# One of every two router row tiles is normalized on GpSimd instead of ScalarE

## The chip, the cores and the metric

One core of a Trainium2 chip. The metric is the device time of one execution in microseconds (us), taken as the median of several executions. Everything is float32.

## The reference, cut to what matters

The input is 4 x 1024 tokens of 256 values. It is layer-normalized, and the result feeds two branches, whose outputs are added to the input:

```python
xn = _layernorm(x, axis=-1)                     # (x - mean) / sqrt(var + eps)
x = x + attn(xn, ...) + ffn(xn, Wr, W1, V1, W2)
# attn: RMS norm, two projections 256 -> 512, a causal convolution of 4 taps, silu,
#       h = exp(d * A) * h + (d * x) * b over 1024 steps (512 channels x 16 states), y = sum(h * c),
#       gate, projection 512 -> 256, plus its own residual
# ffn:
gates = softmax(xn @ Wr)                        # 8 experts
_, inds = top_k(-gates, 2)                      # the two smallest gates of each token
out = (silu(xn @ W1[e]) * (xn @ V1[e])) @ W2[e] # for the two chosen e, weighted by their scores
```

The change concerns the rows `xn` that the router and the experts read.

## The kernel before, in words

**Chunks and units.** The tokens are worked on in 16 chunks of 256. Each chunk has 32 "units" (2 halves of the channels x 16 states). For a unit w, ScalarE computes two exponentials (`exps`, L547 to L555), VectorE one product (`products`, L1133) and two scans (`scan`, L1149), GpSimd once for every two units a product of 128x1024 (`parts`, L758), and TensorE adds these up (`sum_parts`, L850). ScalarE issues the exponentials of unit w + 2 at unit w, GpSimd takes the pair w - 2, w - 1 at an even unit w, and TensorE sums unit w - 4 at unit w.

**Pieces.** All other work is cut into pieces, written by hand into tables (`B_PLACES`, `F_PLACES` and others) that say after which unit of the chunk a piece comes. Every engine walks the same tables in its own instruction order, some kinds of piece some units later (`LATER`): the router pieces `R` come on GpSimd one unit later and on SyncE two units later than on ScalarE and TensorE. An engine executes its instructions strictly in its own order, and a wait holds up everything behind it.

**The router pieces.** Chunk 0 has 18 pieces `R` 0 to 17, at the places `[1, 3, 5, 10, 11, 13, 15, 17, 19, 23, 25, 26, 26, 26, 26, 26, 27, 29]`. Of the 32 row tiles of 128 tokens, piece i (i < 16) handles tiles 2i and 2i + 1:

- ScalarE (L669 to L683) normalizes the two tiles from `xall` into two of the four slots of `tok` (L676), and then copies the turned tiles 2i - 2 and 2i - 1 from the banks H and V into `xT` (L682).
- TensorE (L974 to L991) multiplies the tiles 2i - 4 and 2i - 3 by the router's weights (L982, 8 columns into bank X), and then turns the tiles 2i - 2 and 2i - 1 from `tok` into the banks H and V (L990). It waits for `xn_r`, the count of normalized tiles.
- GpSimd (L776 to L786) computes the residual rows of the tiles 2i and 2i + 1 from the same `xall` (L785).
- SyncE (L467 to L477) stores the two tiles of `tok` to the DRAM tensor `xt` (L473, after `xn_r`) and the two residual tiles to `acc` (L476, after `res_set`).

A slot of `tok` is used again by piece i + 2, which therefore waits until TensorE has turned the tiles of piece i (the bank count of piece i + 1) and until the store of piece i has landed (`xt_out`). A residual slot waits in the same way for `res_out`.

**What follows them.** When all 32 tiles have their 8 logits, VectorE computes gates, choices and slots (pieces RA to RE, L1170 to L1258), and SyncE loads the experts' weights (L480, L483) over the memory of `xall`. Also in chunk 0 the pieces B of chunk 1 are made: ScalarE's taps (L610, L612) and GpSimd's two additions for each of four channel groups (L793, L795; ScalarE's next taps wait for the second), the silu (L617), the projections B3 (L908, L910), B4 (L920, read by ScalarE at L638 and L640).

Of the kernel before, what the change touches and what calls it, by code (L numbers as in the profile page):

```python
# [18 lines left out]
ALU = mybir.AluOpType  # L19
ACT = mybir.ActivationFunctionType  # L20
# [199 lines left out]
def mamba_moe(nc, x, norm_w, skip_wT, in_wT, conv_w, conv_b, wd1T, wd2T, wd2_b, wBCT, A_log, W_D, out_wT,  # L220
# [3 lines left out]
    with ctx:  # L224
# [144 lines left out]
        s_part = sem("s_part")  # L369
        s_sum = sem("s_sum")  # L370
        y_taken = sem("y_taken")
        xn_r = sem("xn_r")
        xTr = sem("xTr")
        lgt = sem("lgt")
# [53 lines left out]
        @block.sync  # L428
        def _(sp):
            def load_quarter(t):  # L430
                sp.dma_start(xall[:, t:t + 8, :], x_rows[t * P:(t + 8) * P, :].rearrange("(t p) d -> p t d", p=P)).then_inc(ld_x[t // 8], 16)

            def load_chunk(c):

                if c >= 1:
                    wait_full(sp, "G", ("B1", 0, c - 1))
                sp.dma_start(xch[:, :, :], x_rows[c * CH:(c + 1) * CH, :].rearrange("(s p) d -> p s d", p=P)).then_inc(ld_xch[c % 2], 16)

            def load_rows(k):

                c, q, n = unit(2 * k)
                if k >= ROW_PAIRS:
                    sp.wait_ge(s_part, k - ROW_PAIRS + 1)
                if q == 0 and n == 0:
                    sp.wait_ge(brow_w, 32 * (c + 1))
                sp.dma_start(bcr[:, k % ROW_PAIRS * 2:k % ROW_PAIRS * 2 + 2, :],
                             brow_d[N * c + n:N * c + n + 2, :].unsqueeze(0).to_broadcast([P, 2, 2 * CH])).then_inc(ld_bc[k % ROW_PAIRS], 16)

            def do(piece):
                kind = piece[0]  # L450
                if kind == "B1" and piece[2] + 1 < CHUNKS:
                    load_chunk(piece[2] + 1)
                elif kind == "B3":
                    c = piece[2]
                    wait_taken(sp, "G", piece)
                    for k in range(2):
                        sp.dma_start(brow_d[N * c:N * (c + 1), k * CH:(k + 1) * CH], tap[N * k:N * (k + 1), 0, :]).then_inc(brow_w, 16)
                    if c == 0:
                        load_rows(0)
                        load_rows(1)  # L460
                elif kind == "T5":
                    c = piece[2]
                    for s, b in enumerate("HG"):
                        t = SUB * c + s
                        wait_taken(sp, b, ("T3", 0, c))
                        sp.dma_start(out_rows[t * P:(t + 1) * P, :], mst[:, s, :]).then_inc(o_out, 16)
                elif kind == "R" and piece[1] < TT // 2:  # L467
                    i = piece[1]
                    if i == 0:
                        sp.wait_ge(zero_set, 1)  # L470
                        sp.dma_start(xt[TOKENS:TOKENS + P, :], empty).then_inc(xt_zero, 16)
                    sp.wait_ge(xn_r, 2 * (i + 1))
                    sp.dma_start(xt[2 * i * P:2 * (i + 1) * P, :].rearrange("(s p) d -> p s d", p=P),  # L473
                                 tok[:, 2 * i % 4:2 * i % 4 + 2, :]).then_inc(xt_out[i % 2], 16)
                    sp.wait_ge(res_set, 2 * (i + 1))
                    sp.dma_start(acc[2 * i * P:2 * (i + 1) * P, :].rearrange("(s p) d -> p s d", p=P),  # L476
                                 resid[i % 2]).then_inc(res_out[i % 2], 16)  # L477
                elif kind == "R" and piece[1] == TT // 2:

                    sp.dma_start(v1[:, :].rearrange("p (e k f) -> p e k f", e=EXPERTS, k=KD), V1.rearrange("e (k p) f -> p e k f", p=P)).then_inc(ld_v1, 16)  # L480
                    sp.wait_ge(xn_r, TT)
                    sp.wait_ge(res_set, TT)
                    sp.dma_start(w1[:, :].rearrange("p (e k f) -> p e k f", e=EXPERTS, k=KD), W1.rearrange("e (k p) f -> p e k f", p=P)).then_inc(ld_w1, 16)  # L483
                elif kind == "MF":

                    sp.wait_ge(idx_set, 2)
                    sp.dma_start(w2[:, :].rearrange("p (e k f) -> p e k f", e=EXPERTS, k=FF // P), W2.rearrange("e (k p) f -> p e k f", p=P)).then_inc(ld_w2, 16)
                elif kind == "CP":
                    t0, t1 = ((0, TT - 2 * SUB), (TT - 2 * SUB, TT - SUB))[piece[1]]
                    wait_landed(sp, ("FC", JT))  # L490
                    wait_landed(sp, ("O3", 1, CHUNKS - 3 + piece[1]))
                    sp.dma_start(out_rows[t0 * P:t1 * P, :], acc[t0 * P:t1 * P, :]).then_inc(o_out, 16)
                elif kind == "LL":
                    wait_landed(sp, ("FC", JT))
                    wait_full(sp, "G", ("FA", JT))
                    sp.dma_start(last, acc[(TT - SUB) * P:TT * P, :].rearrange("(s p) d -> p s d", p=P)).then_inc(ld_last, 16)

            load_chunk(0)

            for done, loads in (  # L500
                (ld_first, [(inw[:, :, :], in_wT.rearrange("(k p) e -> p k e", p=P)),
                            (cw[:, :, :], conv_w.rearrange("(k p) w -> p k w", p=P)), (cb[:, :], conv_b)]),
                (ld_small, [(wbc[:, :, 0:N], wBCT[0].rearrange("(k p) n -> p k n", p=P)),
                            (wbc[:, :, N:2 * N], wBCT[1].rearrange("(k p) n -> p k n", p=P)),
                            (Am[:, :, :], A_log.rearrange("(k p) n -> p k n", p=P)),
                            (wd1[:, :, :], wd1T.rearrange("(k p) r -> p k r", p=P)),
                            (wd2[:, :], wd2T), (db[:, :], wd2_b), (WD[:, :], W_D)]),
            ):
                for dst, src in loads:
                    sp.dma_start(dst, src).then_inc(done, 16)  # L510
            for t in range(0, TT, 8):
                load_quarter(t)
            for dst, src in [(wrt[:, :, :], Wr.rearrange("(k p) e -> p k e", p=P)),
                             (outw[:, :, :], out_wT.rearrange("(k p) d -> p k d", p=P)),
                             (skw[:, :, :], skip_wT.rearrange("(k p) e -> p k e", p=P)),
                             (trim, tri), (csts, cst)]:
                sp.dma_start(dst, src).then_inc(ld_late, 16)
            for piece in prologue():
                do(piece)
            at = places_of("SP")  # L520
            for w in range(UNITS):
                if w % 2 == 0 and w // 2 + 2 < UNITS // 2:
                    load_rows(w // 2 + 2)
                for piece in at[w]:
                    do(piece)
            for piece in epilogue():
                do(piece)
            sp.wait_ge(o_out, 16 * 4)
# [3 lines left out]
        def _(act):  # L532
# [40 lines left out]
            def do(piece):  # L573
# [95 lines left out]
                elif kind == "R":  # L669
                    i = piece[1]  # L670
                    if i < TT // 2:
                        if i >= 2:
                            wait_full(act, "V", ("R", i - 1))
                            act.wait_ge(xt_out[i % 2], 16 * (i // 2))
                        for t in (2 * i, 2 * i + 1):
                            nc.scalar.activation(tok[:, t % 4, :], xall[:, t, :], ACT.Identity, bias=nmr[:, t:t + 1],  # L676
                                                 scale=rstd[:, t:t + 1]).then_inc(xn_r, 1)
                    if 1 <= i <= TT // 2:
                        for k, t in enumerate((2 * i - 2, 2 * i - 1)):
                            wait_full(act, "HV"[k], piece)  # L680
# [62 lines left out]
        def _(pool):  # L743
# [30 lines left out]
            def do(piece):  # L774
                kind = piece[0]
                if kind == "R" and piece[1] < TT // 2:  # L776
                    i = piece[1]
                    if i == 0:
                        pool.wait_ge(stat, STAT_LN[1])
                        for k in range(TT // 8):  # L780
                            pool.wait_ge(ld_x[k], 16)
                    at_least(pool, res_out[i % 2], 16 * (i // 2))
                    for k in range(2):
                        t = 2 * i + k
                        nc.gpsimd.tensor_scalar(resid[i % 2][:, k, :], xall[:, t, :], r1[:, t:t + 1], nmr[:, t:t + 1],  # L785
                                                ALU.mult, ALU.add).then_inc(res_set, 1)  # L786
# [60 lines left out]
        def _(pe):  # L847
# [30 lines left out]
            def do(piece):  # L878
# [95 lines left out]
                elif kind == "R":  # L974
# [10 lines left out]
                    if 1 <= i <= TT // 2:  # L985
                        for k, t in enumerate((2 * i - 2, 2 * i - 1)):
                            wait_free(pe, "HV"[k], piece)
                            pe.wait_ge(xn_r, t + 1)
                            for kd in range(KD):
                                mm = pe.transpose(bank["HV"[k]][:, kd * P:(kd + 1) * P], tok[:, t % 4, kd * P:(kd + 1) * P], idn[:, :])  # L990
                            mm.then_inc(full["HV"[k]], 1)  # L991
# [409 lines left out]
```

## Time and profile before

| | |
|---|---|
| median of 3 executions | 1282.13 us (1279.8 to 1283.07) |
| the profiled execution | 1284.09 us |
| its span, first to last instruction | 1282.3 us |
| mean granted TensorE clock | 0.926 of full speed |
| busy share: TensorE, VectorE, ScalarE, GpSimd | 84%, 91%, 79%, 78% |

PE is TensorE, PEld its weight loads, DVE is VectorE, ACT is ScalarE, POOL is GpSimd, SP is SyncE with its DMA queue. `scr` is the memory that holds `tok`, `xT`, the residual rows and others; `w` on the input side of L676 and L785 is `xall`. Times in the rows are from the start of the span.

### The profile page before, as it was taken

To read this page: it belongs to the slowest core of one execution; us is meant where nothing else is said; L and a number is where in the kernel's file an instruction comes from. 1 tells how busy PE (TensorE), PEld (TensorE's weight loads), DVE (VectorE), ACT (ScalarE), POOL (GpSimd) and SP (SyncE) were. 2 spreads that over 40 slices of the span, in tenths; PEclk is the share of its full clock that TensorE was granted. 3 is DMA by queue.
4 is the path that set the end of the run, shared out by engine and by line. 5 is a ranking of instruction groups with operands and counts; after the bars stand their busy time and mean duration, and the time that the engine had idled before them with its cause. 6 is when DMAs were issued, how large, how long until landed. Compare 5 with 4: busy or idle time off the path is not lost.

```text
span 1282.3 us, 20051 instructions
## 1 busy us (share of the span) xinstructions
PE 1073.0 (84%) x5406; PEld 807.0 (63%) x5406; DVE 1170.8 (91%) x2145; ACT 1013.4 (79%) x2153; POOL 1003.4 (78%) x602
## 2 busy tenths in 40 slices
PE   3379376587998989999989999898999999998766
PEld 2268265465766666676767666676767667675555
DVE  5874899899999999999989899999989899999896
ACT  2797345589898888879888898889888898988862
POOL 1396277678898979888888988989898988989654
PEclk8686597799999999899999999999999999999987
DMA  7467723745554453545545454555545455545436
GB/s 227 143 205 253 267 77 106 231 139 146 147 146 140 141 160 120 150 141 145 146 133 155 121 154 138 146 157 144 146 123 155 135 145 148 155 122 140 126 125 190
DMA packets 87117, 195.08 MB, mean 152 GB/s; under 512 B 11184, under 2 KB 47152, under 8 KB 86928
## 3 DMA queue, kind: packets, MB, share of 16 engines
q1 hardware_dynamic: 69008, 171.18, 41.4%
q0 software_dynamic: 17712, 22.55, 10.6%
q8 instruction: 47, 0.77, 0.2%
q14 instruction: 62, 0.51, 0.1%
q10 hardware_dynamic: 288, 0.07, 0.0%
HBM read 171.22 MB, written 26.48 MB: 154 GB/s over the span
## 4 chain that ended last, share of the span: by engine, by line
PE 32%; ACT 21%; POOL 17%; issue 13%; DVE 12%; DMA 4%; DVEq 0%; POOLq 0%; ACTq 0%
POOL part L763 11%; ACT aexp L554 8%; PE yps L858 7%; PE bankX L1051 5%; DVE hb L1159 5%; PE bankV L1041 4%; PE bankH L1017 4%; DVE bps L1138 4%; DMA acc<-scr,idx 3%; ACT tap L612 3%; ACT L554 2%; PE bankG L898 1%; POOL scr L771 1%; POOL acc L819 1%; POOL tap L793 1%
## 5 line engine op out<-in xcount | busy, mean ns | idle before, releaser
L763 POOL TENSOR_TENSOR part<-hb,bcr 128x1024 f32<-128x1024 f32 x256 | 625.2, 2449 | 147.1 <-DVE hb L1159 102.5
L1159 DVE TENSOR_TENSOR_SCAN hb<-aexp,carry,bps 128x256 f32<-128x256 f32 x768 | 545.6, 733 | 11.4 <-ACT aexp L554 11.4
L554 ACT ACTIVATE aexp<-delta,Am 128x256 f32<-128x256 f32 x1024 | 446.9, 503 | 54.2 <-DVE hb L1159 52.7
L858 PE MATMUL yps<-idn,part 128*128 128x128 f32 x2048 | 300.2, 287 | 92.8 <-POOL part L763 88.4
L858 PEld LDWEIGHTS yps<-idn,part 128*128 128x128 f32 x2048 | 250.9, 148 | 164.9 <-POOL part L763 97.7
L1138 DVE TENSOR_TENSOR bps<-ups,bcr 128x512 f32<-128x512 f32 x512 | 345.2, 674 | 1.1
L1159 DVE TENSOR_TENSOR_SCAN hb<-aexp,bps 128x256 f32<-128x256 f32 x256 | 167.8, 673 | 23.9 <-ACT aexp L554 23.3
L1051 PE MATMUL bankX<-w,scr 128*128 x568 | 143.2, 397 | 21.8 <-ACT scr L703 19.4
L1017 PE MATMUL bankH<-w,scr 128*128 x284 | 137.9, 608 | 2.1 <-issue 2.1
L1041 PE MATMUL bankV<-v,scr 128*128 x284 | 134.2, 595 | 4.7 <-ACT xin L603 3.3
L1051 PEld LDWEIGHTS bankX<-w,scr 128*128 128x128 f32 x568 | 107.8, 198 | 43.0 <-issue 29.8
L819 POOL DMA_INDIRECT acc<-scr,idx x71 | 114.2, 1609 | 22.4 <-ACT scr L713 7.9
L793 POOL TENSOR_TENSOR tap<-tap 128x512 f32<-128x512 f32 x56 | 78.4, 1400 | 10.3 <-ACT tap L612 10.0
L771 POOL DMA_INDIRECT scr<-xt,idx x71 | 72.3, 1018 | 12.4 <-issue 7.4
L1017 PEld LDWEIGHTS bankH<-w,scr 128*128 128x128 f32 x284 | 51.0, 195 | 42.6 <-issue 40.6
L1041 PEld LDWEIGHTS bankV<-v,scr 128*128 128x128 f32 x284 | 48.4, 190 | 40.3 <-issue 40.3
L612 ACT ACTIVATE tap<-xin,cw 128x256 f32<-128x256 f32 x168 | 72.5, 496 | 0.0
L713 ACT ACTIVATE scr<-bankX,meta 128x256 f32<-128x256 f32 x71 | 33.1, 466 | 49.1 <-PE bankX L1051 49.1
L1327 DVE SCALAR_TENSOR_TENSOR scr<-scr,bankH 128x512 f32<-128x512 f32 x71 | 47.5, 669 | 26.3 <-ACT scr L693 26.2
L693 ACT ACTIVATE scr<-bankH 128x512 f32<-128x512 f32 x71 | 41.9, 590 | 27.8 <-PE bankH L1017 27.8
L554 ACT ACT_TABLE_LOAD x48 | 61.6, 1283 | 0.9
L424 POOL TENSOR_TENSOR delta<-delta,y 128x1024 f32<-128x1024 f32 x15 | 35.3, 2355 | 33.3 <-ACT y L650 33.2
(187 smaller groups left out, 1616.9 us busy)
## 6 DMA issues: line engine op xcount, KB each, us to landing
bcr<-brows SPq DMA_DIRECT2D x256, 512.0 KB
w<-in_W SPq DMA_DIRECT2D x2, 4096.0 KB, 21.9
xch<-in_x SPq DMA_DIRECT2D x16, 256.0 KB, 3.8
w<-in_x SPq DMA_DIRECT2D x4, 1024.0 KB, 9.8
xt<-scr SPq DMA_DIRECT2D x16, 256.0 KB, 2.8
acc<-scr SPq DMA_DIRECT2D x16, 256.0 KB, 2.7
v<-in_V SPq DMA_DIRECT2D x1, 4096.0 KB, 14.9
acc<-mst POOLq DMA_DIRECT2D x15, 256.0 KB
```

Source lines behind the costliest of these rows:

```text
L554: nc.scalar.activation(aexp[:, w % EXP_SLOTS, i, :], delta[:, c % 2, e, :], ACT.Exp, scale=Am[:, e, n:n + 1]).then_inc(s_a, 1)
L612: ins = nc.scalar.activation(tap[:, w, :], xin[:, e, w:w + CH], ACT.Copy, scale=cw[:, e, w:w + 1])
L763: nc.gpsimd.tensor_tensor(part[:, slot:slot + 2, :, :], hb[:, state:state + 2, :, :], bcr[:, row:row + 2, CH:2 * CH].unsqueeze(2).to_broad ...
L771: nc.gpsimd.indirect_dma_start(out=tok[:, j % 2, :], out_offset=None, in_=xt, in_offset=bass.IndirectOffsetOnAxis(ap=idx[:, j:j + 1], axis ...
L793: nc.gpsimd.tensor_tensor(tap[:, 0:2, :], tap[:, 0:2, :], tap[:, 2:4, :], ALU.add).then_inc(cvs, 1)
L819: nc.gpsimd.indirect_dma_start(out=acc, out_offset=bass.IndirectOffsetOnAxis(ap=idx[:, j:j + 1], axis=0), in_=tok[:, 2 + j % 2, :], in_off ...
L858: mm = pe.matmul(yps[:, s, i * P:(i + 1) * P], part[:, w % (2 * PART_PAIRS), i, s * P:(s + 1) * P], idn[:, :], start=(n == 0 and s == 0 an ...
L1017: mm = pe.matmul(bank["H"][:, :], xT[:, j % 2, k, :], w1[:, bass.ds(col + k * FF, FF)], start=(k == 0), stop=(k == KD - 1))
L1041: mm = pe.matmul(bank["V"][:, :], xT[:, j % 2, k, :], v1[:, bass.ds(columns[j] + k * FF, FF)], start=(k == 0), stop=(k == KD - 1))
L1051: mm = pe.matmul(bank["X"][:, 0:D], gT[:, k * P:(k + 1) * P], w2[:, bass.ds(columns[j] + k * D, D)], start=(k == 0), stop=(k == FF // P - 1))
L1138: v.tensor_tensor(bps[w % 2][:, :, :], ups[:, :, :], bcr[:, w % (2 * ROW_PAIRS), 0:CH].unsqueeze(1).to_broadcast([P, 2, CH]), ALU.mult).th ...
L1159: v.tensor_tensor_scan(hb[:, w % STATE_SLOTS, i, :], aexp[:, w % EXP_SLOTS, i, :], bps[w % 2][:, i, :], first, ALU.mult, ALU.add).then_inc ...
```

## The change

ScalarE normalizes only tile 2i of a piece. GpSimd normalizes tile 2i + 1, ahead of the two residual tiles of the same piece, after the same two waits for the slot. A new semaphore `xn_p` counts GpSimd's tiles, and those who waited for `xn_r` now wait for both.

```diff
@@ SyncE, piece R
-                    sp.wait_ge(xn_r, 2 * (i + 1))
+                    sp.wait_ge(xn_r, i + 1)
+                    sp.wait_ge(xn_p, i + 1)
                     sp.dma_start(xt[2 * i * P:2 * (i + 1) * P, :].rearrange("(s p) d -> p s d", p=P),
@@ SyncE, the weight loads
-                    sp.wait_ge(xn_r, TT)
+                    sp.wait_ge(xn_r, TT // 2)
+                    sp.wait_ge(xn_p, TT // 2)
@@ ScalarE, piece R
-                        for t in (2 * i, 2 * i + 1):
-                            nc.scalar.activation(tok[:, t % 4, :], xall[:, t, :], ACT.Identity, bias=nmr[:, t:t + 1],
-                                                 scale=rstd[:, t:t + 1]).then_inc(xn_r, 1)
+                        t = 2 * i
+                        nc.scalar.activation(tok[:, t % 4, :], xall[:, t, :], ACT.Identity, bias=nmr[:, t:t + 1],
+                                             scale=rstd[:, t:t + 1]).then_inc(xn_r, 1)
@@ GpSimd, piece R
+                    if i >= 2:
+                        wait_full(pool, "V", ("R", i - 1))
+                        pool.wait_ge(xt_out[i % 2], 16 * (i // 2))
+                    t = 2 * i + 1
+                    nc.gpsimd.tensor_scalar(tok[:, t % 4, :], xall[:, t, :], rstd[:, t:t + 1], nmr[:, t:t + 1],
+                                            ALU.mult, ALU.add).then_inc(xn_p, 1)
                     at_least(pool, res_out[i % 2], 16 * (i // 2))
@@ TensorE, piece R
-                            pe.wait_ge(xn_r, t + 1)
+                            pe.wait_ge((xn_r, xn_p)[k], t // 2 + 1)
```

## Rows read from the trace of the kernel before

**Rows 1.** The page: busy time of each engine over the span

```profile
PE 1073.0 (84%) x5406; PEld 807.0 (63%) x5406; DVE 1170.8 (91%) x2145; ACT 1013.4 (79%) x2153; POOL 1003.4 (78%) x602
```

**Rows 2.** By stretch: busy PE, PEld, DVE, ACT, POOL; clock, DMA share, GB/s

```profile
65.40:85.10 19.70, 13.80 (x91) 12.50 (x89) 15.15 (x29) 18.92 (x45) 19.46 (x18) 0.83 0.52 173
85.10:103.10 18.00, 13.21 (x85) 10.34 (x85) 17.08 (x34) 17.97 (x44) 14.79 (x12) 1.00 0.85 276
103.10:128.10 25.00, 24.54 (x119) 22.81 (x118) 8.76 (x17) 18.45 (x44) 13.62 (x18) 0.52 0.78 244
160.00:240.00 80.00, 54.75 (x311) 48.21 (x309) 79.54 (x132) 42.93 (x84) 59.98 (x33) 0.86 0.31 98
```

**Rows 3.** Timeline of VectorE: start us, us, ..., idle before and releaser

```profile
103.25 0.67 DVE L1138 TENSOR_TENSOR bps<-ups,bcr 128x512 f32<-128x512 f32 x1
122.89 0.69 DVE L1159 TENSOR_TENSOR_SCAN hb<-aexp,bps 128x256 f32<-128x256 f32 x1 [12.60 <-ACT aexp L554]
128.27 0.42 DVE L1172 COPY w<-bankX 128x256 f32<-128x256 f32 x1 [3.51 <-PE bankX L982]
```

**Rows 4.** Timeline of ScalarE, 70 to 117 us

```profile
70.88 0.60 ACT L610 ACTIVATE tap<-xin,cb,cw 128x256 f32<-128x256 f32 x1 [0.75 <-POOL x L795]
73.38 1.08 ACT L676 ACTIVATE scr<-w,nmr,rstd 128x256 f32<-128x256 f32 x2
74.36 0.36 ACT L682 ACTIVATE scr<-bankH 128x256 f32<-128x256 f32 x1
81.74 0.38 ACT L682 ACTIVATE scr<-bankV 128x256 f32<-128x256 f32 x1
92.26 0.36 ACT L682 ACTIVATE scr<-bankV 128x256 f32<-128x256 f32 x1
114.85 1.09 ACT L676 ACTIVATE scr<-w,nmr,rstd 128x256 f32<-128x256 f32 x2 [1.17 <-DMA xt<-scr]
```

**Rows 5.** Line L785: duration ns min/median/max, first and last start us

```profile
L785 POOL TENSOR_SCALAR scr<-w,r,nmr x32: 554/560/577, 55.3 to 119.5; 128x256 f32<-128x256 f32 x32
```

**Rows 6.** Timeline of GpSimd, 70 to 125 us

```profile
70.11 0.73 POOL L795 TENSOR_TENSOR x<-tap 128x256 f32<-128x256 f32 x1
80.61 1.11 POOL L785 TENSOR_SCALAR scr<-w,r,nmr 128x256 f32<-128x256 f32 x2
84.01 1.11 POOL L785 TENSOR_SCALAR scr<-w,r,nmr 128x256 f32<-128x256 f32 x2
106.94 2.19 POOL L785 TENSOR_SCALAR scr<-w,r,nmr 128x256 f32<-128x256 f32 x4
122.95 2.36 POOL L763 TENSOR_TENSOR part<-hb,bcr 128x1024 f32<-128x1024 f32 x1 [2.86 <-PE yps L858]
```

**Rows 7.** Timeline of TensorE, 80 to 128 us

```profile
80.55 0.38 PE L990 MATMUL bankV<-idn,scr 128*128 128x128 f32 x2
85.92 1.97 PE L908 MATMUL bankG<-x,wd 128*128 128x256 f32 x8 [0.73 <-ACT x L617]
90.82 0.38 PE L990 MATMUL bankV<-idn,scr 128*128 128x128 f32 x2
91.04 1.04 PE L858 MATMUL yps<-idn,part 128*128 128x128 f32 x8
102.83 0.44 PE L990 MATMUL bankV<-idn,scr 128*128 128x128 f32 x2 [0.99 <-ACT delta L640]
110.43 1.88 PE L982 MATMUL bankX<-wrt,scr 128*128 128x8 f32 x8 [0.23 <-ACT scr L682]
124.62 0.63 PE L990 MATMUL bankV<-idn,scr 128*128 128x128 f32 x2
```

**Rows 8.** Timeline of SyncE's queue: the loads of the rows b and c

```profile
82.15 0.47 SPq L446 DMA_DIRECT2D bcr<-brows  x1
97.69 2.41 SPq L446 DMA_DIRECT2D bcr<-brows  x2
```

**Rows 9.** The chain of waits: the same projection L908 earlier, in chunk 0's prologue

```profile
25.21 3.68 PE bankG L908 x8
```

More of the change, by code:

```diff
@@ L371, in mamba_moe @@
         y_taken = sem("y_taken")
+        xn_p = sem("xn_p")
         xn_r = sem("xn_r")
```

## The prediction

> **What bounds the kernel now.** The page gives VectorE 91% of the span, the other three about 80% [rows 1]. The change touches 16 pieces between 54 and 122 us, so I read the busy times by stretch. Four stretches differ [rows 2]. From 65.4 to 85.1 us GpSimd is busy for 19.46 of 19.70 us and ScalarE for 18.92: both are full. From 85.1 to 103.1 ScalarE is full (17.97 of 18.00) and GpSimd has 3.2 us left. From 103.1 to 128.1 TensorE is full (24.54 of 25.00) at a granted clock of 0.52, that is at 1.2 GHz, while ScalarE has 6.5 us and VectorE 16 us to spare. After 160 VectorE is full (79.54 of 80). What links the third stretch to the rest is VectorE's first router instruction: it starts at 128.27 after waiting for the last logits on TensorE, and before that VectorE had stood 12.60 us waiting for ScalarE's exponentials, which lie behind the pieces R11 to R15 [rows 3]. So the date that matters is that of the last logits. Whatever it moves by moves VectorE's router work, and since VectorE then stays full, nearly the whole kernel. The question is what the change does to that date.
>
> **What is moved.** 16 instructions leave ScalarE. Two of L676 start 0.98 us ahead of what follows them (73.38 to 74.36 [rows 4]), so each takes 0.49 us of the engine, 7.8 us in all. 16 instructions come to GpSimd. They have the form of L785, a multiply and an add on 128x256 with one input tile; one takes 0.56 us alone [rows 5], and four in sequence take 2.19 [rows 6], so each after the first adds (2.19 - 0.56) / 3 = 0.54, 8.7 us in all. The price of the new instruction is thus known from the trace, with bounds of 0.55 and 0.58 for one alone [rows 5].
>
> A port rule speaks against the move. The 32 instructions L785 stand in stretches with VectorE scanning (to 109 us) and with it silent (110 to 122), and differ by 4% at most, 554 to 577 ns [rows 5]. The Trainium skill ("GPSIMD Engine Reference", Specifications) says that GpSimd's way into SBUF is shared with VectorE and contended when VectorE reads two SBUF inputs; by that rule the moved work would cost more than here. The trace of this stretch does not bear it out, and the kernel says why: scan and product each take one of their two inputs from PSUM.
>
> **Step 1, to R3.** R0 and R1 save ScalarE 0.98 us, but its time there ends in waits for TensorE's projection, so I count nothing. At R2 GpSimd's piece becomes 0.54 longer, and everything behind it in its order moves: the addition L795 from 70.11 [rows 6] to 70.65. ScalarE's next taps wait for exactly that one, 0.75 us in vain, until 70.88 [rows 4]; they start at 71.42. ScalarE's own saving at R2 only lengthens that wait. So ScalarE is 0.54 late, where one would expect it early. R3 gives 0.49 back: +0.05.
>
> **Step 2, R4 and R5: a new wait.** GpSimd has no gap here [rows 2], so R4 begins 2 x 0.54 later than 80.61 [rows 6], at 81.7, and its normalized tile is ready at 82.2. TensorE wanted to turn that tile (tile 9, bank V) at 80.55 [rows 7], and ScalarE to copy it at 81.74 [rows 4]. Now the turn starts at about 82.3 and takes 0.4, the copy starts at 82.75, and the exponentials behind it 0.26 later, at 83.0 instead of 82.0: ScalarE is 1.0 us late at this point, after having lost its savings of R4 and R5 (0.98) in the wait. Queued behind the waiting copy on ScalarE are the exponentials, VectorE's next input and the silu of chunk 1; VectorE loses about 1 us here and regains part, since it had other waits.
>
> **Step 3, R6 and R7.** GpSimd's R5 starts three additions later, 84.01 + 1.6 = 85.6 [rows 6], tile 11 is ready at 86.2. TensorE's R6 turns it by 86.65, then come two sums (x8, spacing 0.88 [rows 7]), so L908 starts at 87.5 instead of 85.92 [rows 7]. From the start of L908 to the end of R7's turn it takes 90.82 + 0.38 - 85.92 = 5.28 us [rows 7], so R7's bank V is ready at 92.8 and ScalarE copies it then, 0.55 later than 92.26 [rows 4].
>
> **Step 4, to the end of B4.** R8 gives 0.49 back: +0.05. GpSimd, 1.3 to 1.7 us late, has its gaps of 3.2 us in this stretch [rows 2] and is no longer in anyone's way: tile 15 is ready at 94.1, TensorE wants it at about 94. TensorE's turn for R9 into bank V waited until 102.83 for ScalarE's last read of B4 [rows 7], and moves with it by +0.05.
>
> **Step 5, R9 to R16.** Here TensorE works without a gap. Each piece costs it logits of 1.87 us and two turns, 2.9 us together. ScalarE's removed instructions (seven, 3.4 us) lie beside that and save nothing, except 0.2 us where TensorE waited 0.23 for a copy [rows 7]. The one wait for a store, 1.17 us until 114.85 [rows 4], delayed no TensorE work: TensorE is full all the same [rows 2]. GpSimd's new waits for `xt_out`: I walked R10 to R15 with landings 2.8 to 4.7 us after issue; the normalized tiles come at 108.3, 109.9, 111.7, 115.2, 117.7 and 119.9, each before TensorE turns it (the last one at 124.62 [rows 7]). The residuals of R15 end about 1 us later than before; the next product on GpSimd waited 2.86 us for TensorE, until 122.95 [rows 6], and covers that. Sum: +0.05 - 0.2, about -0.1 us at the last logits.
>
> **SyncE** waits for GpSimd's tile too, and behind these waits stand the loads of the rows. The tightest: the load at 82.15 [rows 8] moves with the residuals of R4 to 83.75, 5.0 us ahead of its use. In the kernel before the second load of the pair at 97.69 + 2.41 [rows 8] is used at 103.25 without a wait [rows 3], 3.15 us after the end of its issue. So nothing. The weight loads that follow R15 are first used in chunk 2 and stay hidden.
>
> **The sum.** The profiled execution took 1284.09 us; -0.1 gives 1284.0. That execution lies 1.96 above the median of 1282.13, so the forecast for the median is 1282.0. About 0.3% (3.9 us) is what a measurement of this kernel can tell from no change; three executions differ by 3.3 us.
>
> **Rival 1, ScalarE keeps its saving** (0.07). If GpSimd is not late at R2 to R5, the savings R3 to R8 reach B4: 6 x 0.49 = 2.9, with the 0.2 a gain of 3.1: 1279.0. For it: ScalarE is full to 103 [rows 2]. Against it: GpSimd's full stretch, and a row in which ScalarE already waits for L795 [rows 4].
>
> **Rival 2, the TensorE clock drops earlier** (0.14). With the new wait TensorE stands idle from about 80.5 to 82.3 and 85.0 to 86.2. If the clock falls to 1.2 GHz there, L908 takes 3.68 us [rows 9] instead of 1.97 [rows 7], L910 likewise +1.8, two sums +0.9, R7's logits and turns +1.4: 5.8 us. R7's bank V then comes at 98.6, ScalarE waits for it, and B4 and the last logits move by these 5.8 on top of the forecast: 1287.8, slower. If the clock is back after L908 the price is 2.6 and the result 1284.6, which I count as no change; it decides from 3.9 on, when the clock stays down through L910. For it: the clock was at 0.83 in this stretch, so it does fall there [rows 2]. Against: TensorE keeps 14 of 19.7 us of work, and the projections follow at once. I give 0.08 to the full price. The Trainium skill ("TensorE: Matmul & The Clock Gate", What's actually happening) has the slow clock as the default that only activity releases; more idling then makes the drop likelier, which is the direction of this rival.
>
> **Rival 3, the clock stays up through R9 to R16** (0.06). TensorE's 24.54 us [rows 2] of work at half clock would shrink, a piece from 2.9 to about 2.0 us (then ScalarE's copies and TensorE's latencies set it): 7 x 0.9 = 6: 1276, faster. The clock fell there after waits for ScalarE's L640 that the change leaves as they are.
>
> **Rival 4, GpSimd stays late** (0.12). If ScalarE can't take back its lateness since GpSimd's tiles of R7 and R8 come last as well, up to the 4 x 0.54 = 2.2 us of R2 to R5 reaches B4; less the 0.2 of step 5 that makes 1284.1, no change by the bound.
>
> The change does what it says; no case for it. The forecast itself has 0.61. Faster than 1278.3: rival 3 and the tail of rival 1, 0.08. Slower than 1286.0: rival 2 at full price and tails of rival 4, 0.12. Within: 0.80. The range 1278.5 to 1286.5 takes in rivals 1 and 4, the cheaper form of rival 2, and the spread of executions.
>
> **What would show it.** GpSimd's L785 and its new line 0.56 us each; ScalarE's taps at 71.4 with a wait of over 1 us for L795; a new wait for the new line on TensorE at 80 to 82 us and another at 85 to 86; GpSimd busy without a gap to 87; L908 at about 87.5; the last logits at 128.2 within 0.5. Wrong it would be if the first router instruction of VectorE starts before 126 or after 131, if TensorE's clock differs in 84 to 92 or 104 to 126, or if the time moves after 160 us, where I expect nothing.

## The result: slower, and the profile after

The changed kernel takes 1288.88 us (median of 13 executions, 1284.86 to 1293.63) against 1284.36 for the kernel before (13 executions, 1279.8 to 1287.6): ratio 1.0037, 95% interval 1.0024 to 1.0049, that is 4.5 us more. The forecast was 1282.0, no change, with a range up to 1286.5. It was wrong. Of the 6.9 us between forecast and result 2.2 come from the kernel before, whose first 3 executions had a median of 1282.13 and whose 13 have 1284.36; the change itself is the 4.5.

The page of the changed kernel gives nearly the same shares as [rows 1], with ScalarE's 6.9 us less and GpSimd's 8.5 us more; TensorE, which has the same instructions as before, is busy 14 us longer:

```profile
PE 1087.2 (84%) x5406; PEld 818.8 (64%) x5406; DVE 1169.7 (91%) x2145; ACT 1006.5 (78%) x2137; POOL 1011.9 (79%) x618
```

Busy time by stretch, in the columns of [rows 2], first the stretches of the forecast, then 72 to 92 us:

```profile
65.40:85.10 19.70, 13.96 (x69) 12.54 (x68) 13.55 (x26) 15.90 (x41) 19.39 (x20) 0.66 0.40 139
85.10:103.10 18.00, 17.55 (x103) 15.24 (x102) 14.78 (x29) 15.79 (x36) 17.35 (x18) 0.80 0.81 260
103.10:128.10 25.00, 22.23 (x104) 20.30 (x104) 11.66 (x24) 16.55 (x40) 17.70 (x25) 0.56 0.73 233
160.00:240.00 80.00, 55.50 (x308) 48.15 (x309) 79.19 (x132) 45.09 (x87) 59.14 (x32) 0.84 0.29 93
...
72.00:92.00 20.00, 17.49 (x79) 16.45 (x79) 13.06 (x26) 16.68 (x36) 19.77 (x21) 0.50 0.56 183
```

ScalarE, all but full before from 65 to 103 us, now has 6 us of gaps there. From 85.1 to 103.1 TensorE is full instead. And from 72 to 92 us its granted clock was 0.50 throughout, 1.2 GHz; in the kernel before it fell at 73 us and was back at 2.4 GHz from 80 on (the next two lines are of the kernel before):

```profile
72.00:80.00 8.00, 5.22 (x26) 5.22 (x26) 4.88 (x10) 8.00 (x21) 7.84 (x8) 0.57 0.49 162
80.00:92.00 12.00, 10.53 (x72) 8.15 (x72) 9.65 (x20) 11.94 (x25) 10.89 (x10) 1.00 0.64 212
```

**A common clock for the traces.** Executions reach the first product of GpSimd (L763, L766 after) between 52.9 and 54.5 us, whatever the kernel, so dates below that compare traces (30.1, 36.4) are counted from that product: 52.93 in the trace before, 54.12 after. The rows and the dates of the clock stay in us from the start of each span. L is the time from it to VectorE's first router instruction. The timeline of VectorE, after, answers to [rows 3]:

```profile
127.36 0.69 DVE L1168 TENSOR_TENSOR_SCAN hb<-aexp,bps 128x256 f32<-128x256 f32 x1 [12.86 <-ACT aexp L557]
...
133.04 0.42 DVE L1181 COPY w<-bankX 128x256 f32<-128x256 f32 x1 [3.82 <-PE bankX L991]
```

L is 133.04 - 54.12 = 78.9, before it was 128.27 - 52.93 = 75.3. So 3.6 us are there when the last logits are, beside 4.5 in the medians, and VectorE is full after 160 as before. An L comes from one execution. What follows it takes 1154.0 us in the trace before, 1155.4 after, and from 1148.5 to 1157.3 in the twenty traces, so an L can be set against an L, and not taken as a share of a median. Now the three timelines between. ScalarE after (L679 is the kept normalization, L685 the copies), answering to [rows 4]:

```profile
73.23 0.60 ACT L613 ACTIVATE tap<-xin,cb,cw 128x256 f32<-128x256 f32 x1 [1.77 <-POOL x L804]
...
83.24 0.38 ACT L685 ACTIVATE scr<-bankH 128x256 f32<-128x256 f32 x1 [0.74 <-PE bankH L999]
84.91 0.38 ACT L685 ACTIVATE scr<-bankV 128x256 f32<-128x256 f32 x1 [1.29 <-PE bankV L999]
...
96.43 0.38 ACT L685 ACTIVATE scr<-bankH 128x256 f32<-128x256 f32 x1 [2.15 <-PE bankH L999]
96.71 0.38 ACT L685 ACTIVATE scr<-bankV 128x256 f32<-128x256 f32 x1
...
106.64 0.58 ACT L679 ACTIVATE scr<-w,nmr,rstd 128x256 f32<-128x256 f32 x1
```

GpSimd after, with the new line L789, answering to [rows 6]:

```profile
83.51 0.56 POOL L789 TENSOR_SCALAR scr<-w,rstd,nmr 128x256 f32<-128x256 f32 x1
84.05 1.10 POOL L794 TENSOR_SCALAR scr<-w,r,nmr 128x256 f32<-128x256 f32 x2
85.11 2.36 POOL L766 TENSOR_TENSOR part<-hb,bcr 128x1024 f32<-128x1024 f32 x1
87.45 0.56 POOL L789 TENSOR_SCALAR scr<-w,rstd,nmr 128x256 f32<-128x256 f32 x1
```

TensorE after (L999 turns, L867 sums, L991 logits, L917 and L919 the projections of B3), answering to [rows 7]:

```profile
84.22 0.66 PE L999 MATMUL bankV<-idn,scr 128*128 128x128 f32 x2 [1.02 <-POOL scr L789]
84.67 1.91 PE L867 MATMUL yps<-idn,part 128*128 128x128 f32 x8
86.38 1.71 PE L991 MATMUL bankX<-wrt,scr 128*128 128x8 f32 x8
87.94 0.67 PE L999 MATMUL bankH<-idn,scr 128*128 128x128 f32 x2
88.40 0.63 PE L999 MATMUL bankV<-idn,scr 128*128 128x128 f32 x2
88.83 1.91 PE L867 MATMUL yps<-idn,part 128*128 128x128 f32 x8
90.53 2.76 PE L917 MATMUL bankG<-x,wd 128*128 128x256 f32 x8
...
96.23 0.38 PE L999 MATMUL bankV<-idn,scr 128*128 128x128 f32 x2
```

The story can be read off. TensorE waits 1.02 us for GpSimd's tile 9 and ScalarE 1.29 for its turn, as forecast. From then on TensorE has no gap until 96, but works at half clock: sums 1.91 us instead of 1.04, logits 1.71 instead of about 1. So the projection starts at 90.53, 3.4 us later than before on the common clock, and ScalarE, which arrives at R7 in good time, stands 2.15 us for the turns of R7. In ScalarE's queue behind them are the exponentials, B4 and R9.

### The profile page after: what moved, and what is told of

It reads as the page before. It is cut to its first block, busy times and chain, and to the rows that moved or that the text cites. A ratio compares the mean times of both kernels' runs of the same rounds, so it can differ in the third digit from the quotient of the medians.

```text
span 1288.4 us, 20081 instructions
## 1 busy us (share of the span) xinstructions
PE 1087.2 (84%) x5406; PEld 818.8 (64%) x5406; DVE 1169.7 (91%) x2145; ACT 1006.5 (78%) x2137; POOL 1011.9 (79%) x618
## 4 chain that ended last, share of the span: by engine, by line
PE 36%; POOL 21%; ACT 16%; issue 13%; DVE 10%; DMA 3%; DVEq 0%; POOLq 0%; ACTq 0%
POOL part L766 14%; PE yps L867 8%; ACT aexp L557 6%; PE bankX L1060 5%; PE bankH L1026 5%; PE bankV L1050 4%; DVE hb L1168 4%; DVE bps L1147 3%; DMA acc<-scr,idx 2%; ACT tap L615 2%; POOL tap L802 2%; POOL acc L828 2%; PE bankG L917 2%; PE bankG L919 1%; PE bankG L907 1%
## 5 line engine op out<-in xcount | busy, mean ns | idle before, releaser
L766 POOL TENSOR_TENSOR part<-hb,bcr 128x1024 f32<-128x1024 f32 x256 | 625.3, 2452 | 143.8 <-DVE hb L1168 98.6
L867 PE MATMUL yps<-idn,part 128*128 128x128 f32 x2048 | 305.9, 291 | 95.0 <-POOL part L766 91.2
L867 PEld LDWEIGHTS yps<-idn,part 128*128 128x128 f32 x2048 | 257.0, 151 | 167.3 <-POOL part L766 100.1
L1168 DVE TENSOR_TENSOR_SCAN hb<-aexp,bps 128x256 f32<-128x256 f32 x256 | 168.0, 674 | 25.5 <-ACT aexp L557 23.8
L774 POOL DMA_INDIRECT scr<-xt,idx x71 | 72.3, 1019 | 13.3 <-issue 7.7
L696 ACT ACTIVATE scr<-bankH 128x512 f32<-128x512 f32 x71 | 41.9, 589 | 30.2 <-PE bankH L1026 30.1
L425 POOL TENSOR_TENSOR delta<-delta,y 128x1024 f32<-128x1024 f32 x15 | 35.4, 2358 | 33.8 <-ACT y L653 32.8
```

The lines of the kernel that those rows point to most:

```text
L766: nc.gpsimd.tensor_tensor(part[:, slot:slot + 2, :, :], hb[:, state:state + 2, :, :], bcr[:, row:row + 2, CH:2 * CH].unsqueeze(2).to_broad ...
L774: nc.gpsimd.indirect_dma_start(out=tok[:, j % 2, :], out_offset=None, in_=xt, in_offset=bass.IndirectOffsetOnAxis(ap=idx[:, j:j + 1], axis ...
L867: mm = pe.matmul(yps[:, s, i * P:(i + 1) * P], part[:, w % (2 * PART_PAIRS), i, s * P:(s + 1) * P], idn[:, :], start=(n == 0 and s == 0 an ...
L1168: v.tensor_tensor_scan(hb[:, w % STATE_SLOTS, i, :], aexp[:, w % EXP_SLOTS, i, :], bps[w % 2][:, i, :], first, ALU.mult, ALU.add).then_inc ...
```

## The experiments

Three theories were set against each other: GpSimd's load in a full stretch (theory 1), TensorE's wait for GpSimd's tile (theory 2), and TensorE's clock, which stays at 1.2 GHz for longer (theory 3). `busy(n)` in the diffs issues n matmuls of 128x256 into columns of bank X that nothing reads at that time.

All are compared with the kernel before on the same chips; "time" is the median of 12 executions (6 for mid), the ratio is to the kernel before, with its 95% interval. The kernels of a set shared 23 to 35 executions of the kernel before, with medians between 1283.7 and 1284.3.

**load**: GpSimd's extra work alone.

```diff
+                    nc.gpsimd.tensor_scalar(resid[i % 2][:, 0, :], xall[:, 2 * i + 1, :], rstd[...], nmr[...],
+                                            ALU.mult, ALU.add).then_inc(twice, 1)
+                    pool.wait_ge(twice, i + 1)
                     for k in range(2):
```

> The kernel before, with GpSimd's part of the change as a load alone: it computes a tile like the moved one into the first residual slot, where the residual tile then overwrites it; ScalarE keeps both tiles and nobody waits for the extra one. Read as the local time L, from the start of GpSimd's first product to the start of VectorE's first router instruction: 75.3 us before, 78.9 after. If the load of a full GpSimd is the cause (theory 1), L rises by 3 us or more, since here not even ScalarE's saving counters it, and the whole by 3 to 6 us. If the new wait of TensorE for GpSimd's tile is the cause (theory 2), L rises by less than 1.5 us. If TensorE's slow clock is the cause (theory 3), L follows the clock: up by 3 or more only if the granted clock between 72 and 92 us is at 0.5.

1286.22 us, ratio 1.0026 (1.0011 to 1.0041); L 78.1. Slower without any new wait for the tile, by the medians less than the change (2.1 us against 4.5), though the two intervals overlap. L is 2.7 up, a little short of the 3 that theory 1 asked for. The timeline of TensorE shows the path: its sums before B3 wait for GpSimd's product, and then the clock, back since 80.8 us, is at 0.50 from 87.6 to 91.0, in the projection.

```profile
86.71 1.16 PE L862 MATMUL yps<-idn,part 128*128 128x128 f32 x8 [1.92 <-POOL part L764]
87.67 3.56 PE L912 MATMUL bankG<-x,wd 128*128 128x256 f32 x8
```

**wait**: the new wait alone, in its mildest form.

```diff
                             pe.wait_ge(xn_r, t + 1)
+                            if k == 1:
+                                pe.wait_ge(res_set, t)
```

> The kernel before, with the new wait alone: TensorE turns tile 2i + 1 only after GpSimd's first residual tile of piece i, which stands where the change puts its normalized tile. No work is added or moved. Theory 1 (load): no change, L within 1 us of 75.3. Theory 2 (wait): L up by 2 us or more, ScalarE's copy of bank V in R5 at least 0.5 us late. Theory 3 (clock): L up by 2 or more if the clock is at 0.5 in 80 to 92, else within 1.

1284.47 us, ratio 1.0002 (0.9983 to 1.0021); L 76.3. No change. Its first product stands at 54.02, next to that of the changed kernel, so its trace serves below as a second kernel before. TensorE waits 0.2 us for tile 9, its clock came back at about 85 us, and B3 met it:

```profile
87.82 1.97 PE L908 MATMUL bankG<-x,wd 128*128 128x256 f32 x8 [0.20 <-ACT x L617]
```

**save**: ScalarE's saving alone. The normalization of every second tile is left out.

```diff
-                        for t in (2 * i, 2 * i + 1):
+                        t = 2 * i
...
-                                mm = pe.transpose(..., tok[:, t % 4, kd * P:(kd + 1) * P], idn[:, :])
+                                mm = pe.transpose(..., tok[:, (t - k) % 4, kd * P:(kd + 1) * P], idn[:, :])
```

> ScalarE's part alone: it normalizes tile 2i, and tile 2i + 1 is left out of the computation; TensorE turns tile 2i twice and the store writes it twice. All theories: L falls, by 2 to 4 us, as ScalarE's saving of R3 to R8 (2.9 us) reaches the last logits; if the saving is worth nothing even without GpSimd's part, L stays within 1 us of 75.3 and ScalarE was not what bounded this stretch.

1282.3 us, ratio 0.9990 (0.9972 to 1.0008); L 74.8, not the fall of 2 to 4 us of a saving that reaches the end. So even free of charge the moved work is worth at most 3.6 us by the interval, and is not clear of nothing. B4 ends 1.7 us earlier than before, and L is only 0.5 shorter: the rest goes in R9 to R16.

**early, late, mid, r4**: the change for some pieces only, in the order of the runs.

```diff
+        def moved(i):
+            return i < 6          # early; late: i >= 6; mid: 3 <= i < 6; r4: i == 4
```

> The change for the pieces R0 to R5 alone; from R6 on ScalarE keeps both tiles. All three theories place the damage in R0 to R5: L at least as long as after, 78.9 to 81, since R6 to R8 give nothing back, and the whole 4 to 7 us over before. If the damage came later, L is within 1 us of 75.3.

> The change for the pieces R6 to R15 alone; up to R5 ScalarE keeps both tiles. If the damage is done in R0 to R5, L (first product on GpSimd to first router instruction on VectorE; 75.3 before, 78.9 after) is 73.5 to 75.5 and the whole within 2 us of before or faster. If the damage is done later, L is 77 or more.

> The change for R3, R4 and R5 alone, the pieces in which GpSimd has no gap. If these make the loss, L is 78 or more. If GpSimd's extra tile at R0 to R2, ahead of the additions for which ScalarE's taps wait, is needed for it too, L is 76 to 77.5, and within 1 us of 75.3 if those are all of it.

> The change for the piece R4 alone, one tile. GpSimd is late by one addition only, its tile is ready 28.3 us after its first product, TensorE wants it at 27.6. If a short wait there suffices to keep the clock at 0.5 until 36 us or later, L is 77 or more; if not, L is within 1 of 75.3 and the loss needs the lateness of R2 and R3 too.

| | moved | time | ratio, interval | R5 bank V copied | L |
|---|---|---|---|---|---|
| early | R0 to R5 | 1287.6 | 1.0033 (1.0015 to 1.0051) | 30.9 | 79.8 |
| late | R6 to R15 | 1284.83 | 1.0005 (0.9988 to 1.0022) | 29.3 | 75.3 |
| mid | R3 to R5 | 1290.73 | 1.0054 (1.0038 to 1.0070) | 30.1 | 79.3 |
| r4 | R4 | 1282.13 | 0.9993 (0.9974 to 1.0012) | 28.9 | 75.4 |

Three tiles, those of R3 to R5, make the whole loss. By the medians they cost more than the whole change (6.4 us against 4.5), but the intervals overlap. One tile, R4's, makes none: TensorE's wait is then 0.60 us, and the clock comes back as before. The ten tiles of R6 to R15 change nothing that the interval tells from zero: late ends B4 0.9 us before the kernel before, and gives it back at R11, where TensorE, at full clock until then, waits for GpSimd. It is the wait that the forecast had walked through and found covered:

```profile
109.32 0.66 PE L1019 MATMUL bankV<-idn,scr 128*128 128x128 f32 x2 [1.56 <-POOL scr L806]
```

**ahead**: GpSimd has the same work, but the normalized tile of R0 to R10 one unit earlier, apart from the residual tiles.

```diff
+                at[g][:0] = [("N",) + piece[1:] for piece in place if piece[0] == "R" and piece[1] < 11]
```

> The changed kernel, with GpSimd's normalized tile of R0 to R10 taken out of its piece and put one unit earlier on GpSimd, where ScalarE's piece stands; the residual tiles stay. Theory 2 (TensorE waits for GpSimd's tile): the wait goes, L falls to 76 or less. Theory 1 (load): GpSimd has as much to do, L stays above 78. Theory 3: L follows the clock between 72 and 92 us.

1283.71 us, ratio 1.0001 (0.9984 to 1.0017); L 76.8, between what was asked of theory 2 (76 or less) and of theory 1 (above 78). The loss is gone with all 8.7 us of work still on GpSimd: it hangs on where the tile stands in GpSimd's order. TensorE has no wait for the tile, and its clock is back at 83 us, but falls again at 86.6, so that the projection of B3 runs at half clock, and ScalarE waits for the turns of R7 even longer than in the changed kernel:

```profile
86.56 3.58 PE L922 MATMUL bankG<-x,wd 128*128 128x256 f32 x8
...
93.28 0.39 ACT L685 ACTIVATE scr<-bankH 128x256 f32<-128x256 f32 x1 [2.66 <-PE bankH L1004]
```

So neither a projection at half clock nor that wait makes the loss by itself. What ahead lacks is the late start: B3 starts 33.5 us after the first product, 33.0 in the kernel before and 36.4 in the changed one.

**wait5**: the kernel before with one late turn.

```diff
                             pe.wait_ge(xn_r, t + 1)
+                            if i == 5 and k == 1:
+                                pe.wait_ge(s_part, 7)
```

> The kernel before with one wait added and no work moved or added: TensorE turns tile 9 (R5, bank V) only after GpSimd's product of the units 12 and 13, which ends 31.1 us after its first product, where the changed kernel turned it at 30.1 and the kernel before at 27.6. If one late turn makes the loss through TensorE (idle, slow clock, B3 late), L is 77.5 or more and the clock stays at 0.5 until past 34 us; if GpSimd's load is needed, L is under 76.5.

1289.03 us, ratio 1.0041 (1.0026 to 1.0056); L 79.8. A single late turn, nothing moved, costs 5 us. The turn is at 31.7, later than the 30.1 of the changed kernel, so the 5 us are not the change's own share. ScalarE's copy of R5 comes 3 us late (a wait of 3.01 us), TensorE's clock stays at 0.50 from 73 to 93 us, and B3 starts at 38.0.

```profile
73.00:91.00 18.00, 12.19 (x58) 11.42 (x57) 10.26 (x19) 14.95 (x34) 14.28 (x14) 0.50 0.51 181
```

**wait5_warm**: the same late turn with TensorE kept active, by matmuls into unused columns of bank X.

```diff
+                        busy({3: 2, 4: 4}.get(i, 0))
...
+                            busy(7 if i == 5 and k == 1 else 0)
```

> The kernel before with the one late turn of the run before (R5, bank V, ready 31.1 us after GpSimd's first product), and extra matmuls that keep TensorE active until then: two at R3, four at R4, seven between the turns of R5. Wait and loads are those of the run wait5; only TensorE's clock should differ. If the slow clock makes most of that run's loss, the second projection L908 starts at 35 us instead of 38.0 after the first product and L is 77.5 or less (79.8 there, 76.1 with extra matmuls but no wait); if the late turn itself makes it, L is 78.5 or more.

1287.61 us, ratio 1.0018 (1.0001 to 1.0035); L 80.1. The clock was up but for 82.8 to 86.2 us, and B3 started at 36.8 (waiting for the silu on ScalarE) instead of 38.0, taking 1.97 us:

```profile
91.27 1.97 PE L912 MATMUL bankG<-x,wd 128*128 128x256 f32 x8 [1.19 <-ACT x L617]
```

But L did not fall, against what the slow clock as the main cause had expected (77.5 or less); 78.5 or more had been named as the sign that the late turn itself makes the loss. ScalarE was 3.3 us late at R5 (32.6 instead of 29.3 in warm35_before) and 3.3 late at the end of B4, with both tiles still its own and no gap to catch up in. There the slow clock had come on top of a lateness that was already as large. The medians point the other way by 1.4 us, but the two intervals overlap.

**warm35_before, warm35_after**: both kernels with eight such matmuls in R3 to R5.

```diff
+                        busy({3: 2, 4: 4}.get(i, 0))
...
+                            busy(2 if i == 5 and k == 1 else 0)
```

> The kernel before with eight extra matmuls of 128x256 into unused columns (0.49 us each at full clock): two at the start of R3, four at the start of R4, two at R5 between the turns into H and V, all where TensorE is idle or nearly. Needed beside the next run. If the clock is then at 1.0 from 72 us on, L stays 74.5 to 76 and the time within 2 us of before, since the kernel before had the full clock back at 80 us.

> The changed kernel with the same eight. With the clock at 1.0 through R3 to R8 and no extra matmul ahead of B3: if the slow clock is the larger part of the loss, L is at most 1.5 above the run before with the same eight; if GpSimd's lateness is (its tile for R5 and R6 comes last), it is 2 us or more above. The second projection should start 1 to 1.6 us late by the prediction's step 3.

1285.28 us (1.0007, 0.9992 to 1.0021) and 1286.75 us (1.0022, 1.0005 to 1.0040): with these matmuls the change costs 1.5 us by the medians, and the two intervals overlap. L is 76.1 and 78.7, 2.6 apart; 2 or more had been named as the sign that GpSimd's lateness is the larger part of the loss, 1.5 or less that the slow clock is. The condition of both, full clock from R3 to R8, was not met: in warm35_after the clock was at 0.50 from 72.5 to 79.3 and from 89.5 to 93.0 us. It was up at R5 and R6, and another wait came to light that the half clock had covered, for tile 11; then the clock fell in the projection:

```profile
88.71 0.41 PE L1005 MATMUL bankV<-idn,scr 128*128 128x128 f32 x2 [1.60 <-POOL scr L789]
88.96 1.35 PE L867 MATMUL yps<-idn,part 128*128 128x128 f32 x8
90.11 3.30 PE L921 MATMUL bankG<-x,wd 128*128 128x256 f32 x8
```

B3 starts 2.1 us later than in warm35_before, of which the forecast had 1.6.

**warm_before, warm_after, warm_first_after**: more such matmuls, at every piece from R2.

```diff
+                    busy(8 if i == 9 else 3 if 2 <= i <= 16 else 0)     # warm_first_after: 3 if 2 <= i <= 8 else 0
```

> The kernel before with extra matmuls of 128x256 into unused columns of bank X, three at the start of the pieces R2 to R16 and eight at R9, to keep TensorE active. They cost TensorE some 50 x 0.25 us = 13 us at full clock, mostly in idle time up to 103 us. If they hold the clock at 1.0 in 103 to 128 us, the pieces there shrink from 2.9 to 2.3 us and L falls by 2 to 4; if the clock falls all the same, they cost at half clock 3 x 0.5 us per piece and L rises by 8 or more.

> The changed kernel with the same extra matmuls. Theory 3 (clock): with the clock held at 1.0 in 72 to 92 us the difference to the kernel before with the same matmuls shrinks to under 1 us in L. Theories 1 and 2 (GpSimd's load, the wait for its tile): the difference stays 2 us or more at full clock.

> The changed kernel with the extra matmuls at R2 to R8 alone, where its clock was at 0.5 from 72 to 92 us. If the slow clock there makes half of the loss and GpSimd's lateness the other half, L is 76.5 to 78 (after: 78.9, before: 75.3). If the clock there is all of it, L is 75.5 or less; if it is nothing, L is 79 or more.

1282.86 us (0.9983, 0.9968 to 0.9998), 1284.92 us (1.0007, 0.9992 to 1.0021) and 1287.47 us (1.0030, 1.0017 to 1.0042); L 73.5, 75.4 and 79.4. Each extra matmul took 0.49 us at full clock, not the 0.25 expected. Between the first two the change costs 2.1 us, and 2.0 in L, the least that had been named for theories 1 and 2 (under 1 for the clock); warm_first_after came out where the clock in R2 to R8 is worth nothing (L of 79 or more). But these comparisons are not clean: in both changed kernels the three matmuls of R6 stand ahead of B3, behind the late tile, and the clock was not held from 72 to 92 us (0.89 and 0.85, against 1.00 in warm_before).

**warm9, warm9_late, warm9b**: such matmuls from R9 on only.

```diff
+                    busy(8 if i == 9 else 3 if 10 <= i <= 16 else 0)    # warm9b: 1 instead of 3
```

> The kernel before with the extra matmuls from R9 on alone (8 at R9, 3 at each of R10 to R16), none up to R8. In the run with all of them B4 ended 0.8 us later than before and L was still 1.9 shorter. If that lateness came from the early ones, L is 71.5 to 73.5 here and the time 2 to 4 us under before. If the clock falls at R9 without the early ones, L is over 80.

> The same extra matmuls, with the change for R6 to R15 alone. With TensorE at full clock from R9 on, ScalarE's two normalizations of a piece may lie on the path again, which one on GpSimd would shorten: if so L is 0.5 to 1.5 below the run with the same matmuls and the pieces unchanged. If GpSimd's tile then comes last, L is longer than there.

> The kernel before with eight extra matmuls at R9 and one instead of three at each of R10 to R16. If one is enough to hold the full clock, L falls below the 72.4 of the run with three, to 70 to 71.5, as 14 x 0.49 us leave TensorE's order; if the clock falls again, L is 74 to 77.

1281.38 us (0.9977, 0.9964 to 0.9989), 1283.23 us (0.9988, 0.9976 to 0.9999) and 1285.73 us (1.0010, 0.9992 to 1.0027); L 72.4, 72.3 and 75.0. warm9, the kernel before with 29 matmuls whose results nobody reads, beats both kernels: 3 us under before. It holds the clock where the kernel before had 0.52 [rows 2], and one matmul per piece does not:

```profile
103.00:126.00 23.00, 22.83 (x170) 21.51 (x169) 9.46 (x19) 17.67 (x44) 14.06 (x18) 1.00 0.76 248
```

```profile
103.00:128.00 25.00, 23.73 (x142) 22.15 (x140) 9.87 (x20) 17.86 (x44) 13.81 (x18) 0.73 0.74 234
```

The change for R6 to R15 adds nothing to warm9: its median is 1.9 us higher with overlapping intervals, its L the same.

## Why the prediction was wrong, step by step

The dates from the first product, in us; "forecast" is what its steps added to the trace before:

| | before | wait | after | forecast | after - before | after - wait |
|---|---|---|---|---|---|---|
| ScalarE's taps after L795 | 17.9 | 18.5 | 19.1 | +0.54 | +1.2 | +0.6 |
| ScalarE copies bank V, R5 | 28.8 | 29.6 | 30.8 | +1.0 | +2.0 | +1.2 |
| TensorE starts B3 (L908) | 33.0 | 33.8 | 36.4 | +1.6 | +3.4 | +2.6 |
| ScalarE copies bank V, R7 | 39.3 | 40.1 | 42.6 | +0.55 | +3.3 | +2.5 |
| ScalarE starts R9 | 49.8 | 50.5 | 52.5 | +0.05 | +2.8 | +2.0 |
| first router instruction (L) | 75.3 | 76.3 | 78.9 | -0.1 | +3.6 | +2.7 |

The kernel wait, which moves nothing, shows that single traces of unchanged work differ by up to 0.9 here; against it the shares of the loss stand out.

**What is moved** was right: L789 takes 548 to 573 ns, L679 590 alone. The port rule played no part, as forecast: L794, the residual tiles, takes 548 to 578 ns, as L785 did.

**Steps 1 and 2** were right in mechanism and, against wait, in size (against the trace before both are about twice the forecast): taps 0.6 late, R5's copy 1.2 late, TensorE waiting 1.02 us for L789 where 1.8 was foreseen. Step 1 left out that R0's tile is late too: TensorE turned R1's bank V at 57.16, 0.3 later than before on the common clock.

**Step 3 is the one that failed.** It had TensorE go from R5's turn through sums, logits and turns to B3, and on to R7, with durations from rows at full clock, and so R7's copy 0.55 late. TensorE did this work at half clock, in 90.53 - 84.22 = 6.3 us up to B3, and R7's copy was 2.5 to 3.3 late. The tile 11, on which step 3 had TensorE wait, was ready at 88.0 (87.45 + 0.56), just as TensorE came to it. This gives an estimate of the clock's share. At full clock TensorE would have been early, would have turned tile 11 at 88.1, and with 0.25 for the turn and 0.88 for the sums B3 would have started at about 89.2 instead of 90.53; B3 itself would have taken 1.97 instead of 2.76. That is 2.1 us of the 4.2 by which R7's turns ended late; step 3 had 1.6. ScalarE had 1.1 us to spare there (its copy in the kernel before is at 92.26, the turn's end at 91.20), so by this estimate 2.1 of the 3.3 us at R7's copy are the clock's. Two signs that the forecast had named for being wrong came: the first router instruction after 131 (133.04, or 131.8 on the clock of the trace before), and a changed clock between 84 and 92.

**Rival 2** is nearest to what happened, with 0.14 and only 0.08 at full price. It had the clock fall in the new idle time. In fact the clock was down already, from 73 us in the kernel before and 72 in the changed one, and what changed is that it came back at 92 instead of 80. The mean clock of 0.83 from 65.4 to 85.1 us [rows 2] said that there was a time at half clock in it, from 73 to 80 us; I read the mean and didn't ask which piece stood in that time. In all four traces in which TensorE waits 1 us or more for R5's tile with no extra matmuls (after, early, mid, wait5) the clock stays down until 92 to 93 us; with a wait of 0.6 us or less (before, r4, wait, load, save, ahead, late) it is back at 80 to 85.5. wait5 adds nothing but the wait, so there the wait is the cause; in the changed kernel that is consistent with all traces and not shown alone. The date scatters without a wait too: 80 in before, 85 in late, which are the same kernel up to R5.

**Step 4** was right on its own: R8 gives 0.5 back (2.5 to 2.0). **Step 5** was right that ScalarE's savings in R9 to R16 are worth nothing (save, late), and wrong by 0.8 at the end: B4's end to the first router instruction took 26.3 us instead of 25.5, since TensorE was at half clock there from R9 on to the last logits (the sums behind R9's turn took 1.92 us instead of 1.25, the last logits 1.71 instead of 1.41). **Rival 4**, GpSimd stays late, holds part of the truth: at full clock tile 11 is late by 1.6 us (warm35_after). **Rival 1** can be had only by leaving the work out, and then brings 1.8 us by the medians instead of its 3.1. **SyncE** was forecast to cost nothing, from the load behind R4. The load that came late is an earlier one: behind R2's stores it was issued at 69.27 instead of 66.91, and VectorE waited for it:

```profile
73.63 0.70 DVE L1147 TENSOR_TENSOR bps<-ups,bcr 128x512 f32<-128x512 f32 x1 [0.93 <-DMA bcr<-brows]
```

ScalarE's wait for L804 lies beside it, and I can show no part of L that hangs on it.

**What stays open.** How the 4.5 us divide between ScalarE's and TensorE's lateness and the slow clock. Four comparisons were to tell, and by L none shows the clock as the larger part: wait5_warm keeps all of L, warm_first_after too, and of the 3.6 us of L 2.6 are left in the pair warm35 and 2.0 in the pair warm, while by the medians 1.5 and 2.1 of 4.5 are left. But all of them carry the cost of the extra matmuls, and in each changed kernel the clock still fell somewhere. In wait5_warm ScalarE's own lateness of 3.3 us passes to the end in full; in the changed kernel it was 1.2 us against wait, and the savings of R6 to R8, 1.5 us, could have repaid it. So the argument is that the loss went over TensorE's late B3, and that the slow clock made between half and two thirds of the lateness at R7, by the estimate at step 3; it is not shown by a run that changes only the clock. Nor is the 0.9 us between 3.6 in L and 4.5 in the medians located; by the scatter of what follows L it may be nothing.

## What to carry to other kernels

Before work is moved to an engine, look at where in its order the result is made and who waits for it: all the work on GpSimd, with the tiles of R0 to R10 one unit earlier, cost nothing, and three tiles in the full stretch cost 6 us. When a step is costed on TensorE, take the granted clock of that very stretch in slices of a few us, and ask of each new wait whether it lies in a time at half clock. And where TensorE runs at half clock on a path that sets the end, useless matmuls can be worth their time: here 29 of them gained 3 us, and 15 of them gained nothing (warm9b).

## What was not expected of the hardware

TensorE was busy for 17.49 of 20 us between 72 and 92 us in the changed kernel, up to 90.5 with turns, sums and logits, and its granted clock stayed at 0.50; it rose at 92.3, in the projection of 128x256 matmuls. From 103.1 to 128.1 us the kernel before was at 0.52 with 24.54 of 25 us busy [rows 2]. With three matmuls of 128x256 more per piece it was 1.00, with one 0.73. Such a float32 matmul took 0.49 us at full clock. The kind of matmul does not settle the date either: in the kernel before the clock rose at 79.9 us in the logits of R5, 13 us after its last 128x256 matmul, and in warm35_before it fell at 82.5 us among the extra ones.

The forecast's citation of the Trainium skill ("TensorE: Matmul & The Clock Gate", What's actually happening), that the slow clock is the default and activity releases it, gave the direction of rival 2 rightly. The extra matmuls of warm9, 1.00 instead of 0.52, agree with it. TensorE's busy time did not tell it here: 24.54 of 25 us at 0.52.
